# AdaLN-conditioned FFN on one core: rounding the weight from a constant that ScalarE writes in two bytes, with VectorE adding and GpSimd only subtracting

## The reference

```python
xm = x * cmask[:, :, None]
h = gelu(einsum('bct,bch->bht', xm, W_sess[ids]) + b_sess[ids][:, :, None])
o = (einsum('bht,hs->bst', h, W2) + b2[None, :, None]) * tmask[:, None, :]
w_scale = 448 / max(|weight|, EPS);  x_scale = 57344 / max(|o|, EPS)
w_q = (weight * w_scale).astype(float8_e4m3fn)
x_q = (o * x_scale).astype(float8_e5m2)
out = x + einsum('bsk,nk->bsn', x_q, w_q) / x_scale / w_scale + bias
```

## Time and profile before

| | us |
|---|---|
| median of 3 runs | 833.17 (832.89 to 833.23) |
| profiled execution | 833.1 |
| its span | 831.3 |
| TensorE busy | 825.8 |
| GpSimd busy | 511.8 |
| VectorE busy | 479.5 |
| ScalarE busy | 345.9 |

### The profile page before, as it was taken

How to read it: one execution, slowest core, us unless ns; L and a number is a source line. 1 busy time by engine, 2 the same in 40 slices (tenths; PEclk the granted TensorE clock), 3 DMA queues, 4 the chain that set the end, 5 groups by cost and what they waited for, 6 DMA issues and landing times.

```text
span 831.3 us, 10181 instructions
## 1 busy us (share of the span) xinstructions
PE 825.8 (99%) x3568; PEld 479.9 (58%) x3568; DVE 479.5 (58%) x499; ACT 345.9 (42%) x372; POOL 511.8 (62%) x238
## 2 busy tenths in 40 slices
PE   9999999999999999999999999999999999999998
PEld 5777777776767676765444444444444444444444
DVE  6989889788888888888553232323232323232322
ACT  7999999988888888973100000000000000000000
POOL 2899999899999999995983242424242423232322
PEclk9999999999999999999999999999999999999999
DMA  7988999877777877657974868686868686868682
GB/s 258 322 321 321 367 339 353 301 285 296 284 289 303 305 267 301 253 187 246 298 295 119 282 214 282 210 285 212 280 213 280 214 283 214 279 213 282 215 248 107
DMA packets 75008, 220.77 MB, mean 266 GB/s; under 512 B 37594, under 2 KB 40930, under 8 KB 55778
## 3 DMA queue, kind: packets, MB, share of 16 engines
q1 hardware_dynamic: 74080, 219.30, 74.5%
q10 hardware_dynamic: 898, 1.09, 0.4%
HBM read 143.04 MB, written 69.21 MB: 255 GB/s over the span
## 4 chain that ended last, share of the span: by engine, by line
PE 99%; issue 0%; POOL 0%; DVE 0%; ACT 0%; POOLq 0%
PE ps_h L1071 53%; PE ps_h L980 22%; PE ps_o L995 11%; PE ps_o L1011 8%; PE ps_o L1007 4%; PE ps_o L934 1%; PE ps_h L1047 0%; PE ps_o L1071 0%; PE ps_o L980 0%; PE ps_o L1065 0%; POOL time L518 0%; PE ps_o L940 0%; PE ps_h L1052 0%; DVE o_and_max L881 0%; ACT x_sb L702 0%
## 5 line engine op out<-in xcount | busy, mean ns | idle before, releaser
L1071 PE MATMUL ps_h<-wqT,x_sb 128*128 128x512 bf16 x1920 | 413.7, 378 | 0.2 <-ACT x_sb L702 0.2
L1071 PEld LDWEIGHTS ps_h<-wqT,x_sb 128*128 128x128 fp8e5 x1920 | 187.7, 98 | 224.4 <-ACT x_sb L702 0.3
L528 POOL TENSOR_TENSOR xl<-x_sb,xh 128x1024 fp32r<-128x1024 f32 x62 | 149.5, 2411 | 16.3 <-ACT xh L607 16.3
L980 PE MATMUL ps_h<-xh,whl 128*128 128x512 f32 x508 | 150.3, 417 | 0.4
L569 POOL TENSOR_TENSOR x_sb<-x_sb,bias_sb 128x2048 f32<-128x2048 f32 (+1 forms) x15 | 66.7, 4447 | 131.7 <-DMA x_sb<-in_x 131.7
L569 POOL TENSOR_TENSOR h<-h,bias_sb 128x2048 f32<-128x2048 f32 (+1 forms) x15 | 66.7, 4443 | 122.7 <-DMA h<-in_x 122.7
L881 DVE SCALAR_TENSOR_TENSOR o_and_max<-ps_h,scales,h 128x512 f32<-128x512 f32 (+1 forms) x59 | 44.0, 746 | 136.2 <-PE ps_h L1071 136.2
L881 DVE SCALAR_TENSOR_TENSOR o_and_max<-ps_h,scales,x_sb 128x512 f32<-128x512 f32 x59 | 44.2, 750 | 133.4 <-PE ps_h L1071 133.4
L980 PEld LDWEIGHTS ps_h<-xh,whl 128*128 128x128 f32 x508 | 94.2, 188 | 42.0 <-issue 21.7
L765 DVE SCALAR_TENSOR_TENSOR o_and_max<-ps_o,b_sb,steps 128x1024 f32<-128x1024 f32 (+1 forms) x65 | 82.2, 1264 | 29.0 <-PE ps_o L1011 27.1
L755 DVE TENSOR_TENSOR hl<-ps_h,hh 128x1024 fp32r<-128x1024 f32 x63 | 76.8, 1219 | 13.4 <-ACT ps_h L614 13.3
(11 more groups left out here) (101 smaller groups left out, 657.2 us busy)
## 6 DMA issues: line engine op xcount, KB each, us to landing
x_sb<-in_x SPq DMA_DIRECT2D x44, 1024.0 KB, 5.7
masked_out<-o_and_max SPq DMA_DIRECT2D x32, 1024.0 KB, 6.8
o_in<-masked_out SPq DMA_DIRECT2D x32, 1024.0 KB, 8.9
out<-o_and_max SPq DMA_DIRECT2D x27, 1024.0 KB, 5.1
wqT<-in_L_ffn_weight SPq DMA_DIRECT2D x23, 684.0 KB, 8.3
wt<-in_L_ffn_weight SPq DMA_DIRECT2D x40, 384.0 KB, 5.5
h<-in_x SPq DMA_DIRECT2D x14, 1024.0 KB, 7.2
whl<-split_w SPq DMA_DIRECT2D x18, 256.0 KB, 6.0
```

Of the source, the lines that this page charges most:

```text
L528: pool.tensor_tensor(xl[:, u % 2, :], x_cols(u), xh[:, u % 2, :].bitcast(fp32), ALU.subtract)\
L980: mm = nc.tensor.matmul(to[:, cols], whl[:, b % SLOTS_W, rows], xs[:, u % 2, cols], start=(k == 0), stop=(k == 2))
L1071: mm = nc.tensor.matmul(bank, q[:, k // 2, :, k % 2], wq[:, n, k, cols], start=(k == 0), stop=(k == KT - 1))
```

## The change

Rounding takes its constant from the magnitude of the weight itself in place of its power of two. ScalarE writes |weight| x 2^20 x scale in bf16 (`wc`) with Abs; VectorE raises it to at least 1.5 x 2^-6 x 2^20 (`w_floored`) and then computes weight x scale + wc straight from the loaded chunk (`w_added`); GpSimd subtracts wc. The scale that ScalarE uses is a new one, `w_up`.

With it: `QUANT` is 27, so 34 chunks are early and 9 late, and unit 27 also splits h1. A buffer of `wt` is free when VectorE has added, so the loads wait on `w_added`. In unit 62 VectorE does all of chunk 34; before it did the exponents of chunk 35 there and the rest behind the five cuts. ScalarE does chunk 36 ahead of the widenings. `CHUNK_BEHIND` is (2, 4, 5, 6, 7).

```diff
-    ROUND_AT = 1.5 * 2.0 ** 20
+    ROUND_AT = 2.0 ** 20
-    SPLIT_H1 = [u for u in range(2, 27)]
+    SPLIT_H1 = [u for u in range(2, 28)]
-    QUANT = SCANS + 2
+    QUANT = SCANS + 3
-    CHUNK_BEHIND = range(4, 12)
+    CHUNK_BEHIND = (2, 4, 5, 6, 7)
...
@@ sync, in the unit loop
                     if i >= 3:
-                        sp.wait_ge(w_scaled, i - 2)
+                        sp.wait_ge(w_added, i - 2)
                     load_chunk(i)
@@ gpsimd, round_chunk
-                pool.wait_ge(w_round_ready, i + 1)
-                pool.tensor_tensor(v, v, c, ALU.add).then_inc(w_added, 1)
                 pool.wait_ge(w_added, i + 1)
                 pool.tensor_tensor(wqT[:, CHUNK_AT[i]], v, c, ALU.subtract).then_inc(w_rounded, 1)
...
-            for i in late[0:2]:
+            for i in late[0:3]:
...
-            for i in late[2:6]:
+            for i in late[3:7]:
...
-            for i in late[6:]:
+            for i in late[7:]:
@@ scalar, scale_chunk
-                act.activation(ws[:, i % 2, 0:chunk_cols(i)], wt[:, at:at + chunk_cols(i)], ACT.Copy, scale=w_scale)\
-                   .then_inc(w_scaled, 1)
+                act.activation(wc[:, i % 2, 0:chunk_cols(i)], wt[:, at:at + chunk_cols(i)], ACT.Abs, scale=w_up)\
+                   .then_inc(w_raised, 1)
...
+            scale_chunk(EARLY_CHUNKS + 2)
...
             for i in range(EARLY_CHUNKS + 2, CHUNKS):
-                scale_chunk(i)
+                if i > EARLY_CHUNKS + 2:
+                    scale_chunk(i)
                 if UNITS - QUANT + 2 <= i + 3 < CHUNKS:
-                    act.wait_ge(w_scaled, i + 1)
+                    act.wait_ge(w_added, i + 1)
@@ vector
+            def add_round_at(i):
+                c, at = wc[:, i % 2, 0:chunk_cols(i)], i % 3 * CHUNK
+                dve.wait_ge(w_raised, i + 1)
+                dve.tensor_scalar(c, c, 1.5 * E4M3_MIN_NORMAL * ROUND_AT, None, ALU.max).then_inc(w_floored, 1)
+                dve.wait_ge(w_floored, i + 1)
+                dve.scalar_tensor_tensor(ws[:, i % 2, 0:chunk_cols(i)], wt[:, at:at + chunk_cols(i)], w_scale, c,
+                                         ALU.mult, ALU.add).then_inc(w_added, 1)
...
                 if 0 <= u - QUANT - 1 < EARLY_CHUNKS + 1:
-                    exponents(u - QUANT - 1)
-                if 0 <= u - QUANT - 1 < EARLY_CHUNKS:
-                    round_at(u - QUANT - 1)
+                    add_round_at(u - QUANT - 1)
...
             late = range(EARLY_CHUNKS, CHUNKS)
-            round_at(late[0])
             quantize(1, 1, True, slice(0, T))
...
             for i in late[1:4]:
-                exponents(i)
-                round_at(i)
+                add_round_at(i)
```

More of the change, by code:

```diff
@@ L11, in adaln_ffn @@
     fp32r = mybir.dt.float32r
-    u16 = mybir.dt.uint16
     ALU, ACT, AX = mybir.AluOpType, mybir.ActivationFunctionType, mybir.AxisListType
@@ L30, in adaln_ffn @@
     E4M3_MAX, E5M2_MAX, EPS = 448.0, 57344.0, 1e-12
-    EXPONENT = 0x7F80
     E4M3_MIN_NORMAL = 2.0 ** -6
-    ROUND_AT = 1.5 * 2.0 ** 20
+    ROUND_AT = 2.0 ** 20
     assert C == P and UPB == 2 and HT == 2 and weight.shape == (P, WCOLS)
@@ L47, in adaln_ffn @@
     SLOTS = 5
-    CHUNK, CROWS = 768, 3
+    CHUNK = 768
     CHUNKS = -(-WCOLS // CHUNK)
-    QUANT = SCANS + 2
+    QUANT = SCANS + 3
     EARLY_CHUNKS = UNITS - 3 - QUANT
@@ L120, in adaln_ffn @@
         o_max = sb("o_max", [P, UNITS + 1], fp32)
-        scales = sb("scales", [P, 10], fp32)
+        scales = sb("scales", [P, 11], fp32)
         w_pmax, w_rec, w_scale, w_inv = (scales[:, k:k + 1] for k in range(4))
-        o_pmax, o_amax, o_rec, o_scale, o_inv, y_scale = (scales[:, k:k + 1] for k in range(4, 10))
+        o_pmax, o_amax, o_rec, o_scale, o_inv, y_scale, w_up = (scales[:, k:k + 1] for k in range(4, 11))
         wqT = sb("wqT", [P, WCOLS], bf16)
@@ L146, in adaln_ffn @@
         ws = sb("ws", [P, 2, CHUNK], fp32)
-        wE = sb("wE", [P, CROWS * (CHUNK // CROWS + 2)], u16)
         wc = sb("wc", [P, 2, CHUNK], bf16)
@@ L250, in adaln_ffn @@
         wt_loaded = [sem(f"wt_loaded{r}") for r in range(3)]
-        w_scaled = sem("w_scaled")
-        w_exponent = sem("w_exponent")
-        w_round_ready = sem("w_round_ready")
+        w_raised = sem("w_raised")
+        w_floored = sem("w_floored")
         w_added = sem("w_added")
@@ L299, in adaln_ffn @@
         o_row = ps_h[:, 1, 0:P]
[L301 to L307, removed]
         @block.sync
@@ L627, in scale_chunk @@
                 if i == 0:
-                    act.wait_ge(w_scale_ready, 1)
+                    act.wait_ge(w_scale_ready, 2)
                 if i >= 2:
@@ L771, in scan_o @@
                    .then_inc(o_scanned, 1)
[L773 to L777, removed]
-                    dve.wait_ge(w_round_ready, i)
-                dve.tensor_scalar(exponent_rows(i), v, EXPONENT, None, ALU.bitwise_and).then_inc(w_exponent, 1)
-            def round_at(i):
-                dve.wait_ge(w_exponent, i + 1)
-                dve.tensor_scalar(wc[:, i % 2, 0:chunk_cols(i)], exponent_rows(i).bitcast(bf16), E4M3_MIN_NORMAL,
-                                  ROUND_AT, ALU.max, ALU.mult).then_inc(w_round_ready, 1)
+            def add_round_at(i):
[5 more added lines that the diff above has]
+                                         ALU.mult, ALU.add).then_inc(w_added, 1)
             def scan(s):
@@ L796, in weight_scale @@
                 dve.wait_ge(scale_step, 1)
+                dve.tensor_scalar(w_up, w_rec, E4M3_MAX * ROUND_AT, None, ALU.mult).then_inc(w_scale_ready, 1)
                 dve.tensor_scalar(w_scale, w_rec, E4M3_MAX, None, ALU.mult).then_inc(w_scale_ready, 1)
-                dve.wait_ge(w_scale_ready, 1)
+                dve.wait_ge(w_scale_ready, 2)
                 dve.reciprocal(w_inv, w_scale).then_inc(scale_step, 1)
@@ L902, in _ @@
                        .then_inc(y_ready, 1)
-                if y in CHUNK_BEHIND and 4 + CHUNK_BEHIND.index(y) < len(late):
+                if y in CHUNK_BEHIND:
                     i = late[4 + CHUNK_BEHIND.index(y)]
-                    exponents(i)
-                    round_at(i)
+                    add_round_at(i)
             def step2(i, last):
```

## The result

The changed kernel takes 848.38 us (847.76 to 848.72, 4 runs) against 833.03 (832.82 to 833.23, 4 runs) before: a ratio of 1.0183, with a 95% interval of [1.0166, 1.0201], slower by 15.4 us. The forecast was 839.1 us, with a range of 835.2 to 842.8. The profiled execution took 848.08, its span 846.3, so 15.0 more than the span before.

A forecast was written before the change was run, and what follows sets the result against it. The prediction took TensorE, busy for 99% of the span, to bound the kernel. It summed 833.1 - 0.2 (split unit) + 0.5 (last chunk in the loop) + 5.7 (waits for transpositions) = 839.1 us, with a range of 835.2 to 842.8.

The forecast's parts named there:

- the held wait: Between the stages, SyncE's last chunk load waits for VectorE's addition of chunk 35, delaying transpositions TensorE needs: +5.7 us.
- Rival A: Between the stages, the queue doesn't hold batch 1's transposition, which lands before TensorE wants it: 833.4 us; chance 10%.
- the scale-and-add: VectorE's new pass over a chunk's 768 columns takes 1.02 us, in a straight line between 256 and 1024 columns.
- the split unit: In the first stage, one more unit splits h1, 27 in place of 26: -0.2 us.
- I count 0: In the first stage, the chunk arithmetic isn't on TensorE's path and costs nothing: 0 us.
- the maximum: VectorE's new pass over 768 bf16 in place takes 0.45 us, between half of a 553 ns pass and that pass.
- the cover: In the first stage, VectorE's 28.9 us of waits ahead of masking, over 63 units, cover 0.3 us more per unit.
- the second gap: In the second stage, TensorE waits 2.7 us ahead of batch 2 for the transposition of its q.
- rival B: Between the two transpositions things move in 10.4 us, so TensorE waits once, 3.0 us: 836.4 us; chance 15%.
- rival C: TensorE's clock falls in the waits, and products behind the gaps take 0.43 us; chance 10%.
- the late chunks: In the second stage, nine late chunks are covered before batch 0's products with the last 512 columns: 0 us.
- the last chunk in the loop: At unit 62 VectorE does all of chunk 34, not only an exponent pass, delaying stage two: +0.5 us (0.25 to 0.85).

The follow-up runs named there:

- e6: The kernel before, with only a wait added: SyncE's last chunk load waits until VectorE has the constant of chunk 36; 842.00 us, 1.0108.
- e1: The changed kernel with chunk 38 loaded from ScalarE's queue behind the cuts, so SyncE doesn't wait for VectorE's addition of chunk 35; 839.36 us, 1.0077.
- e7: e1's kernel with VectorE's two chunk passes behind its pass for `hl` in each unit, in place of ahead of it; 837.55 us, 1.0046.
- e4: The changed kernel with 28 idle products in TensorE's list ahead of the wait for batch 1's transposition; 846.77 us, 1.0166.
- e8: e1's kernel with ScalarE writing three padded rows into `ws`, and the maximum reading these and writing a flat `wc`; 834.00 us, 1.0016.
- e10: e7's kernel with one chunk fewer in the unit loop (33), and chunk 37's load moved to ScalarE's queue too; 832.08 us, 0.9994.

## Why the prediction was right and wrong

Of the 15.0 us between the profiled executions 6.4 lie ahead of stage two, where the sum had 0.3, and 8.6 behind its first product, where it had 5.7.

**Right: the held wait, its place and its release.** SyncE was forecast to go on at before-time 389.1, behind five cuts, the quantization of batch 1 and one chunk. It did at 395.25 - 6.4 = 388.9. The order behind it, the landing in a full queue, and a first gap ended by the transposition of x_sb came as described. Rival A (no wait) falls with the gap of 6.4 us and with e6 (9.2 us).

**Right: the scale-and-add** (1.02 forecast; 1.02 in the unit loop, 1.05 on average). **Right: the split unit**, -0.2 forecast: `hl` of unit 28 starts 0.26 us earlier against before than that of unit 27.

**Wrong: "I count 0" for the arithmetic.** With the term for the last chunk it was 6.6 us (e1), the larger part of the error. Two sub-steps failed. First, the maximum was sized from the 553 ns pass between 0.28 and 0.55, as if it depended on its columns alone. That row is from padded rows to flat, the new pass flat to flat. Alone it takes 0.35; behind the start of a pass of GpSimd it is held, here to 0.56 to 1.84 us in the loop, and it is GpSimd's pass that says how long. The trace of before had the sign, in its only flat chunk, the last: 512 columns took 1.61 us, and ended 0.15 behind GpSimd's pass, where 768 in rows take 0.55:

```profile
421.34 1.61 DVE L784 TENSOR_SCALAR wc<-wE 128x512 bf16<-128x512 bf16 x1
```

```profile
421.10 1.70 POOL L537 TENSOR_TENSOR wqT<-ws,wc 128x768 bf16<-128x768 f32 x1
```

Second, the cover: the 28.9 us that VectorE idles lie ahead of the masking passes and were taken as slack of the whole unit. TensorE needs `hl`, which stands behind the chunk. Of before, `hl` of one unit reads

```profile
246.44 1.22 DVE L755 TENSOR_TENSOR hl<-ps_h,hh 128x1024 fp32r<-128x1024 f32 x1
```

and TensorE's next unit

```profile
247.81 1.41 PE L980 MATMUL ps_h<-xh,whl 128*128 128x512 f32 x4
```

It ends at 247.66, and TensorE starts at 247.81, 0.15 behind it. The changed kernel has the same 0.14 (201.93 and 202.07), so before TensorE already started on `hl`; in e7, where it doesn't, 0.55 us lie between. From the start of the masking pass to that of `hl` VectorE takes 3.90 us before, and in the change 3.98 in one unit (202.21 to 206.19), which costs nothing, and 4.44 in the next (196.27 to 200.71), which costs 0.28. So the slack of a unit is more than 0.08 us and, by my estimate from 4.44 - 3.90 - 0.28, about 0.26, not the 28.9/63 = 0.46 of the prediction. The prediction did name the price, "35 units would cost up to 0.3 each", and took it for excluded; 17 pairs of 0.28 and more, and a held last chunk, are what came.

**Wrong size: the wait, 8.7 to 9.0 us in place of 5.7.** The transposition landed 14.0 us behind the release (395.25 to 409.3), not 10.4. The store, the last ahead of it in the queue, landed at 396.10 + 8.8 = 404.9, 9.7 us behind the release, where 10.4 - 2.9 = 7.5 were taken; the transposition followed 4.4 behind it, where 2.9 were taken for latency and transposing. From 395.2 to 409.3 the DMA engines moved, by the five stretches with 122, 284, 345, 267 and 212 GB/s, 3.5 MB: 251 GB/s on average, where the sum assumed 271 to 380, and 0.6 MB more than the 2.9 MB counted (2.6 ahead of it and its own 0.3). Of these 0.39 are ScalarE's second chunk load, which went out at 400.83 on its own queue and landed at 408.8; the sum counted only the first. The other 0.2 to 0.3 may be the o_in issued at 401, which landed at 411.8; that isn't shown, nor why the rate was low. A gap of 6.4 instead of 3.0 followed. (The sum's lower bound for the waits, 3.8, doesn't follow from the numbers beside it: 397.9 + 13.1 - 406.85 is 4.2. It changes nothing here.)

**Wrong: the second gap; right in part: rivals B and C.** No 2.7 us wait for the transposition of batch 2 came; it landed at 413.31 + 8.2 = 421.5, just ahead of TensorE at 421.8. TensorE waited once, as rival B has it, but not for B's reason and at twice its price: 12.2 us lay between the two landings, not 10.4. TensorE arrived late by the longer first gap and by the clock, whose fall in the waits is rival C. It fell in the first, to 0.50, and cost 1.6 (e4) to 2.0 us (12.41 - 10.37). Together 6.4 + 2.0, and 0.2 of rounding and modelled ends, make 8.6, against the 8.7 between the profiled executions of the change and e1. The sum had no term for the clock. The upper end of the range, 842.8, takes in C, and the 0.43 us of a product behind a gap, twice the 0.216 of the earlier trace rows, goes with it: both were the author's estimates, and no run shows a clock that falls in a second wait. The change showed 11 products in 4.29 us, 0.39 each, behind the first gap.

**Right: the late chunks.** Nothing is lost behind 421.82.

**Right: the last chunk in the loop**, +0.5 forecast (0.25 to 0.85): the wait for the scale is 0.8 us in the change and in e8, where the maximum isn't held. Part of it is again holding (1.73 us for a scale-and-add in e8). In e10, which takes this chunk out and also has `hl` first, the wait is gone, and the median is 1.9 us below e8's.

## What to carry to other kernels

How much an engine idles in total tells nothing about the slack of one of its results: subtract the end of that result from the start of its first user, unit by unit. Where that is the same small time in every unit (0.14 us here), the user is already following it. When a VectorE pass changes its layout or type, compare it with a row of the same layout and look at what GpSimd runs beside it; a pass of 0.35 us alone took 1.01 here in every second unit. And a wait that moves to a later event on an in-order queue must be priced with everything queued behind it arriving at once; here it cost 9.0 us.
